# The low products of the next head's keys and values as 64-row tiles, with a chunk's halves in two PSUM banks

## What is computed

```
x = layernorm(x + self_attention(x))        # 16 heads of 16, 4 key/value groups, per sequence
x = layernorm(x + cross_attention(x, ctx))  # 8 heads of 128; all 1792 queries against all 6000 keys
x = layernorm(x + ffn(x))                   # 256 -> 1024 -> 256, ternary weights, exact gelu

# cross attention, for one head h
q = x @ Wq[:, h];  k = ctx @ Wk[:, h];  v = ctx @ Wv[:, h]      # 1792x128, 6000x128, 6000x128
sim = (q @ k.T) * 128 ** -0.5
sim = (sim - mean(sim)) * 1.5 + mean(sim)
out[:, h] = softmax(sim) @ v
```

## Time and profile before

| what | us |
|---|---|
| median of three executions | 2318.58 |
| profiled execution, its own time | 2320.05 |
| its span | 2318.2 |
| TensorE busy (28710 matmuls) | 2264.4 |
| VectorE busy | 2010.6 |
| GpSimd busy | 1893.1 |
| ScalarE busy | 1866.0 |

### The profile page before, as it was taken

How to read it: one execution, slowest core, us unless ns; L and a number is a source line. 1 busy time by engine, 2 the same in 40 slices (tenths; PEclk the granted TensorE clock), 3 DMA queues, 4 the chain that set the end, 5 groups by cost and what they waited for, 6 DMA issues and landing times.

```text
span 2318.2 us, 67173 instructions
## 1 busy us (share of the span) xinstructions
PE 2264.4 (98%) x28710; PEld 2025.3 (87%) x28710; DVE 2010.6 (87%) x2194; ACT 1866.0 (80%) x2220; POOL 1893.1 (82%) x1145
## 2 busy tenths in 40 slices
PE   7999999999999999999999999999999999999997
PEld 4568998899989998999889998999889998999885
DVE  7888888888889888888888888888898888988876
ACT  4357888888888888888888888888888888888854
POOL 8675888888878888888878897888878887899942
PEclk9999999999999999999999999999999999999999
DMA  6410000000000000000000000000000000010310
GB/s 201 155 38 15 7 4 13 4 7 6 11 6 5 7 13 4 6 4 7 13 4 7 4 13 4 6 7 4 13 4 6 7 4 7 4 47 7 110 59 33
DMA packets 34858, 50.79 MB, mean 22 GB/s; under 512 B 2304, under 2 KB 27392, under 8 KB 34560
## 3 DMA queue, kind: packets, MB, share of 16 engines
q1 hardware_dynamic: 34560, 46.46, 6.4%
HBM read 30.99 MB, written 15.47 MB: 20 GB/s over the span
## 4 chain that ended last, share of the span: by engine, by line
PE 70%; POOL 16%; DVE 5%; issue 4%; ACT 3%; POOLq 0%; ACTq 0%; DVEq 0%
PE psum L403 27%; POOL e_lo L1549 11%; PE psum L429 9%; PE psum L427 9%; PE psum L431 9%; PE psum L546 4%; PE psum L536 4%; POOL e_hi L1543 3%; DVE run_max L1045 3%; ACT ring L818 2%; PE psum L672 2%; PE psum L449 1%; PE psum L717 1%; PE psum L699 1%; PE psum L553 1%
## 5 line engine op out<-in xcount | busy, mean ns | idle before, releaser
L1549 POOL TENSOR_TENSOR e_lo<-ring,e_hi 128x1024 f16<-128x1024 f32 (+1 forms) x665 | 1389.5, 2105 | 197.0 <-ACT ring L833 168.4
L1045 DVE TENSOR_TENSOR run_max<-psum,run_max 128x1024 f16<-128x1024 f32 (+1 forms) x616 | 738.2, 1198 | 201.8 <-ACT ring L818 200.7
L818 ACT ACTIVATE ring<-psum 128x1024 f32<-128x1024 f32 (+1 forms) x672 | 674.4, 1004 | 181.5 <-PE psum L403 121.9
L1066 DVE SCALAR_TENSOR_TENSOR ring<-ring,psum 128x1024 f32<-128x1024 f32 (+1 forms) x672 | 792.6, 1186 | 0.7 <-PE psum L639 0.7
L403 PE MATMUL psum<-qx_hi,k_hi 128*128 128x256 f16 x2632 | 718.4, 273 | 13.9 <-DVE run_max L1045 7.7
L427 PE MATMUL psum<-v_main,e_hi 128*128 128x129 f16 x4032 | 717.7, 219 | 1.1 <-POOL e_lo L1549 1.1
L429 PE MATMUL psum<-v_main,e_hi 128*128 128x128 f16 x4032 | 718.3, 221 | 0.0
L403 PE MATMUL psum<-qx_hi,k_lo 128*128 128x256 f16 x2632 | 718.1, 273 | 0.0
L403 PE MATMUL psum<-qx_lo,k_hi 128*128 128x256 f16 x2632 | 718.0, 273 | 0.0
L431 PE MATMUL psum<-v_main,e_lo 128*128 128x129 f16 x4032 | 716.3, 218 | 0.0
L833 ACT ACTIVATE ring<-ring 128x1024 f32<-128x1024 f32 (+1 forms) x672 | 695.9, 1036 | 1.3 <-DVE ring L1066 0.8
(11 more groups left out here) (193 smaller groups left out, 2768.8 us busy)
## 6 DMA issues: line engine op xcount, KB each, us to landing
o_scratch<-o_buf SPq DMA_DIRECT2D x56, 128.0 KB, 1.9
raw<-o_scratch SPq DMA_DIRECT2D x14, 512.0 KB, 4.0
stage<-in_ctxT SPq DMA_DIRECT2D x6, 500.0 KB, 3.9
stage<-in_ctxT SPq DMA_DIRECT2D x12, 250.0 KB, 4.7
w_scratch<-wall SPq DMA_DIRECT2D x1, 2304.0 KB, 11.0
wall<-w_scratch SPq DMA_DIRECT2D x6, 384.0 KB, 3.2
x<-in_xT SPq DMA_DIRECT2D x4, 448.0 KB, 6.5
res<-in_x SPq DMA_DIRECT2D x1, 1792.0 KB, 15.8
```

Of the source, the lines that this page charges most:

```text
L818: a.activation(ring[:, f % SLOTS, 0:n], pair(f)[:, 0:n], ACT.Copy).then_inc(s_kept, 1)
L1045: ins = v.tensor_tensor(run_max[:, 0:n], pair(f)[:, 0:n], run_max[:, 0:n], ALU.max)
L1066: v.scalar_tensor_tensor(slot, slot, LIFT, psum[:, 6, 0:QB].unsqueeze(1).broadcast_to([P, t, QB]), ALU.add, ALU.subtract).then_inc(s_sub, 1)
L1549: g.tensor_tensor(e_lo[f % NEL][:, 0:n], slot, e_hi[f % NEH][:, 0:n], ALU.subtract).then_inc(s_lo, 1)
```

## The change

Keys: a chunk of 512 columns is made as two halves of 256 (`HC`). The products with `whi`, `wlo` and `wshi` are done once for each half. The product with `wslo` uses 64 rows of the array: rows 0 to 63 for the first half, rows 64 to 127 for the second. So that the high part of the context lies in the right rows, `ctx_s` is stacked the other way round in every second 256 keys (low parts in rows 0 to 63), and `wslo` holds the low weights in both halves of its rows, in place of the zeros. Values: of the four key tiles of a group, tiles 0 and 1 use rows 0 to 63, and tiles 2 and 3 use rows 64 to 127.

Where `two_banks(n, s)` holds (in the heads, at steps from 2 on, for full groups), the halves go to two banks: bank 7 and the output bank that the present block doesn't use. The two 64-row products stand next to each other. Elsewhere both halves are in bank 7, the two 64-row products are apart, and the second one waits for the end of the first (`s_rows`). ScalarE and VectorE read the two banks in two instructions each. TensorE waits for the output's store before it uses the borrowed bank (`s_oev`), and for the side tasks' end before a block's first `attend` (`s_free`); ScalarE stores the output earlier in its step, ahead of `keep_scores`. GpSimd works on context blocks of 1024 keys in place of 1000.

```diff
-CH = 1000
+CH = 1024
+HC = KC // 2
...
+        def two_banks(n, s):
+            what, index, h = side_of(n, s)
+            return what in ("k", "v") and n >= 0 and s >= 2 and tiles_of(index) == GT
+        def side_half(n, half):
+            return psum[:, (4 + (n + 1) % 2, 7)[half], 0:HC]
...
+                def key_product(banks, h, c, number=None):
                     whi, wlo, wshi, wslo = [wpack[h % 2][:, 4 + j, :] for j in range(4)]
-                    n = cols_of_keys(c)
-                    for x, (w, y) in enumerate(((whi, ctx_hi), (whi, ctx_lo), (wlo, ctx_hi),
-                                                (wshi, ctx_s), (wslo, ctx_s))):
-                        mm = pe.matmul(psum[:, bank, 0:n], lhsT=w, rhs=y[:, c * KC:c * KC + n],
-                                       start=(x == 0), stop=(x == 4))
+                    one = banks[0] == banks[1]
+                    def product(half, lhsT, y, start=False, stop=False, rows=None):
+                        k0, n = c * KC + half * HC, min(HC, cols_of_keys(c) - half * HC)
+                        of = slice(0, P) if rows is None else rows
+                        at_row = {} if rows is None else {"tile_position": (rows.start, 0)}
+                        return pe.matmul(psum[:, banks[half], one * half * HC:one * half * HC + n], lhsT=lhsT[of],
+                                         rhs=y[of, k0:k0 + n], start=start, stop=stop, **at_row)
+                    product(0, whi, ctx_hi, start=True)
+                    product(1, whi, ctx_hi, start=not one)
+                    if one:
+                        product(0, wslo, ctx_s, rows=rows_of(0)).then_inc(s_rows, 1)
+                    for half in range(2):
+                        product(half, whi, ctx_lo)
+                    for half in range(2):
+                        product(half, wlo, ctx_hi)
+                    if one:
+                        pe.wait_ge(s_rows, number)
+                        product(1, wslo, ctx_s, rows=rows_of(1))
+                    for half in range(2):
+                        mm = product(half, wshi, ctx_s, stop=one and half == 1)
+                    if not one:
+                        for half in range(2):
+                            mm = product(half, wslo, ctx_s, rows=rows_of(half), stop=True)
                     return mm
...
+                    def low(i):
+                        of = rows_of(i // 2)
+                        return pe.matmul(out_of(i), lhsT=ctx_s[of, keys_of(i)], rhs=wslo[of], start=False, stop=True,
+                                         tile_position=(of.start, 0))
+                    if one:
+                        for i in range(tiles_of(g)):
+                            whole(i)
+                            if i == 2:
+                                pe.wait_ge(s_rows, number)
+                            mm = low(i)
+                            if i == 1:
+                                mm.then_inc(s_rows, 1)
+                    else:
+                        for first in range(2):
+                            whole(first)
+                            whole(first + 2)
+                            low(first)
+                            mm = low(first + 2)
                     return mm
...
                     pe.wait_ge(s_free, number)
+                    if two_banks(n, s) and n > 0:
+                        pe.wait_ge(s_oev, n * QT + past * NQB * QT)
+                    banks = (4 + (n + 1) % 2, 7) if two_banks(n, s) else (7, 7)
...
                             pe.wait_ge(s_oev, n_at * QT - QT)
+                        if s == 0 and n >= 1:
+                            pe.wait_ge(s_free, number)
                         attend(n * NGRP + s, past * NQB * NGRP, past * HEAD_SIDES)
...
                         exp_half(weights)
+                    if s == 1 and n > 0:
+                        store_output(n - 1)
                     if f + LEAD < NF_ALL:
                         keep_scores(f + LEAD)
...
-                    if s == 1 and n > 0:
-                        store_output(n - 1)
...
-                for c in (7, 11):
-                    run(g.memset(wall[64:P, :, c, :], 0.0))
...
-                        run(g.tensor_tensor(wall[0:64, :, c + 3, :], rest[0:64], wall[0:64, :, c + 2, :],
-                                            ALU.subtract))
+                        run(g.tensor_tensor(wall[:, :, c + 3, :], rest, wall[:, :, c + 2, :], ALU.subtract))
...
-                        s_low = ctx_s[64:P, c0:c0 + CH]
-                        run(g.tensor_tensor(s_low, st[64:P, 1, 0:CH], s_low, ALU.subtract))
+                        for k0 in range(0, n, KC):
+                            for k, of in ((k0, slice(64, P)), (k0 + HC, slice(0, 64))):
+                                x = min(HC, n - k)
+                                s_low = ctx_s[of, c0 + k:c0 + k + x]
+                                run(g.tensor_tensor(s_low, st[of, 1, k:k + x], s_low, ALU.subtract))
```

More of the change, by code:

```diff
@@ L46 @@
 WA_N = WA_V + NG * DH_S
-CH = 1000
+CH = 1024
+NCH = -(-NKEY // CH)
 W12 = D * FF // P
@@ L224, in build @@
                  halves(INNER, Wk), halves(INNER, Wv)]
-        tasks += [halves(CH, ctxT[:, c * CH:(c + 1) * CH]) for c in range(NKEY // CH)]
+        tasks += [halves(min(CH, NKEY - c * CH), ctxT[:, c * CH:min((c + 1) * CH, NKEY)]) for c in range(NCH)]
         def maxima_bank(u):
@@ L265, in build @@
         s_side, s_half, s_free = sem("b_side"), sem("b_half"), sem("b_free")
+        s_rows = sem("b_rows")
         side16 = psum[:, 7, 0:QB // 2].bitcast(F16)
@@ L319, in build, with one_bank, rows_number @@
         HEAD_SIDES = side_number(NQB, 0) - side_number(0, 0)
+        def two_banks(n, s):
+            what, index, h = side_of(n, s)
+            return what in ("k", "v") and n >= 0 and s >= 2 and tiles_of(index) == GT
+        def one_bank(n, s, task):
+            return task[0] in ("k", "v") and not two_banks(n, s)
+        def rows_number(n, s):
+            return NGRP + sum((m, t) <= (n, s) and one_bank(m, t, task) for m, t, task in SIDES)
+        HEAD_ROWS = rows_number(NQB, -1) - rows_number(0, -1)
+        def side_half(n, half):
+            return psum[:, (4 + (n + 1) % 2, 7)[half], 0:HC]
         def v_of(h, g):
@@ L529, in norm_transposes, with rows_of @@
                     mm.then_inc(l_t, 1)
-                def key_product(bank, h, c):
+                def rows_of(half):
+                    return slice(64 * half, 64 * half + 64)
+                def key_product(banks, h, c, number=None):
                     whi, wlo, wshi, wslo = [wpack[h % 2][:, 4 + j, :] for j in range(4)]
-                    n = cols_of_keys(c)
-                    for x, (w, y) in enumerate(((whi, ctx_hi), (whi, ctx_lo), (wlo, ctx_hi),
-                                                (wshi, ctx_s), (wslo, ctx_s))):
-                        mm = pe.matmul(psum[:, bank, 0:n], lhsT=w, rhs=y[:, c * KC:c * KC + n],
-                                       start=(x == 0), stop=(x == 4))
+                    one = banks[0] == banks[1]
[21 more added lines that the diff above has]
+                            mm = product(half, wslo, ctx_s, rows=rows_of(half), stop=True)
@@ L538, in key_product, with value_product, out_of, keys_of @@
                     return mm
-                def value_product(bank, h, g):
+                def value_product(banks, h, g, number=None):
                     whi, wlo, wshi, wslo = [wpack[h % 2][:, 8 + j, :] for j in range(4)]
[L542 to L547, removed]
+                    one = banks[0] == banks[1]
+                    def out_of(i):
+                        return psum[:, banks[i // 2], (i if one else i % 2) * DH:(i if one else i % 2) * DH + DH]
+                    def keys_of(i):
+                        return slice((g * GT + i) * P, (g * GT + i + 1) * P)
+                    def whole(i):
+                        for x, (y, w) in enumerate(((ctx_hi, whi), (ctx_hi, wlo), (ctx_lo, whi), (ctx_s, wshi))):
+                            pe.matmul(out_of(i), lhsT=y[:, keys_of(i)], rhs=w, start=(x == 0), stop=False)
+                    def low(i):
[16 more added lines that the diff above has]
+                            mm = low(first + 2)
@@ L565, in start_task @@
                     if what == "k":
-                        pe.wait_ge(s_staged, 3 + min(-(-(index + 1) * KC // CH), NKEY // CH))
-                        key_product(7, 0, index).then_inc(st_full, 1)
+                        pe.wait_ge(s_staged, 3 + -(-(index + 1) * KC // CH))
+                        key_product((7, 7), 0, index, index + 1).then_inc(st_full, 1)
                     else:
@@ L614, in side @@
                     pe.wait_ge(s_free, number)
+                    if two_banks(n, s) and n > 0:
+                        pe.wait_ge(s_oev, n * QT + past * NQB * QT)
+                    banks = (4 + (n + 1) % 2, 7) if two_banks(n, s) else (7, 7)
+                    order = rows_number(n, s) + past * HEAD_ROWS
```

(30 more changed lines are left out.)

11 lines of the change are left out of this document (6 added, 5 removed).

## The result

The changed kernel takes 2384.01 us (median of four executions, 2383.74 to 2385.48) against 2319.36 for the kernel before. The ratio is 1.0277 (95% interval 1.0264 to 1.0289): slower by 64.7 us. The forecast was 2373.0, +54.4 us, and 2384 lies inside its range of 2346 to 2388. The direction and the mechanism held; the sum was 10 us short. A head that holds no loop jump grew by 6.96 to 7.06 us (from its first `attend` to the next head's); the forecast was 6.5.

A forecast was written before the change was run, and what follows sets the result against it. The prediction took TensorE to bound the kernel, with each round trip into row tiles costing 0.19 us; its terms summed to 54.4 us, giving 2373.0 us from a median of 2318.58, range 2346 to 2388.

The forecast's parts named there:

- products in the heads: Key chunks and value groups in the heads: 4.6 + 13.7 + 21.6 + 4.6 us slower, from round trips into row tiles.
- self attention and values before the first head: Products standing alone before the heads: 3.5 us more for 12 key chunks, 4.2 us for 9 value groups.
- evacuations: Split ScalarE and VectorE copies out of two banks: 0.31 us once per head where line 536 waits, 2.2 us in all.
- store, s_oev, s_free, s_rows: The output's store moved earlier and TensorE's new waits before borrowed banks, blocks and rows: cost 0.
- rival C: Pairs of 64-row products run in turn, not side by side: 13.6 us on top of the forecast, 2386.6; chance 0.05.
- The bound: Time added on TensorE inside a head lands on the span one for one; ScalarE or VectorE time is free without deadlines.
- The price of a trip: Leaving the plain array for row tiles and returning costs TensorE 0.18 to 0.19 us; 0.19 taken.
- Rival B: No charge for 64-row tiles, so pairs win: 10.5 us faster, 2308.1; chance 0.08.
- Before the first head: Nine value groups alone, partly filling TensorE's gap of about 0.7 us: some 0.85 per two steps, 4.2 us in all.

The follow-up runs named there:

- e1_full_rows: The changed kernel with each 64-row product done on all 128 rows, everything else kept: 2327.18 us, ratio to before 1.0036.
- e2_one_trip: The changed kernel, but a two-bank value group does all 128-row products first, then its four 64-row ones, entering the tiles once: 2368.74 us, ratio 1.0209.
- e6_before_key64: The kernel before, with only the last product of each key chunk on rows 0 to 63; no halves, pairs or second bank: 2338.31 us, ratio 1.0075.
- e3_same_rows: The changed kernel with both products of a pair on the same rows, leaving out the second half's low-weight term: 2394.77 us, ratio 1.0331.
- e5_alone_full: The changed kernel with the 64-row products that stand alone done on all 128 rows, pairs kept on row tiles: 2355.65 us, ratio 1.0152.
- e7_store_late: The changed kernel with the output's store back at its old place, after the exponentials of step 1: 2406.04 us, ratio 1.037.
- e4_unrolled: The changed kernel with TensorE's hardware loop over heads 2 to 5 written out: 2375.2 us, ratio 1.0242.
- e9_before_unrolled: The kernel before with only TensorE's loop over heads 2 to 5 written out: 2315.83 us, ratio 0.9984.

## Why the prediction was right, and where it was short

The sum of the prediction and what the traces show, in us:

| term | forecast | measured | from |
|---|---|---|---|
| products in the heads | 44.5 | 50.7 | lengths of the groups, 49.2, and 0.011 for the product after each of 136 |
| self attention and values before the first head | 7.7 | 8.1 | first `attend` of head 0, 211.46 - 203.37 |
| evacuations | 2.2 | -0.4 | what is left; the wait for the keys' low part got 0.4 shorter |
| store, s_oev, s_free, s_rows | 0 | 0 | no such wait in the view of waits |
| jump of TensorE's loop | 0 | 5.3 | last block of head 3 and first of head 4, against those of other heads |
| clock at the end | 0 | 1.7 | half clock for 3.4 us from 2364.1, in this profiled execution, not in that of the kernel before |
| sum | 54.4 | 65.4 | spans, 2383.6 - 2318.2 |

The forecast's range reached 2388 for rival C's sake, not for the loop's. That 2384 still lies in it, with 7.0 us for which the sum had no term, is in part luck.

**The bound.** It held, nearly one for one, that time added on TensorE lands on the span. From e1_full_rows to the changed kernel the product groups in the heads cost 49.1 us more and the heads grew by 47.8; most of the rest came out of old waits for low parts. Before the heads it was 9.1. The two give 56.9, the medians 56.8.

**The price of a trip: right mechanism, size a little low.** I took 0.19 us from 32-row tiles. The changed kernel shows, from the start of one product to the next (the trace has them to the ns), 0.152 into the tile where 0.056 is due (entry 0.096), 0.159 out of it (exit 0.103), and 0.067 for the next product (0.011): 0.21, and e2_one_trip 0.213. I had seen the 0.01 and named it, and left it out of the sum. The heads have 301 trips; 0.023 more for each is 6.9 us, about the missing 6.2.

Since the price of 0.213 doesn't depend on what is done in the tiles, the best unit of this change, a key chunk as a pair, can save 0.107 and still loses 0.104. The value group needs two trips to save twice 0.053. The products that stand alone save nothing, and cost half of the whole.

**Rival B.** The switch has a price, 0.21 us a trip (e2_one_trip, e6_before_key64), so rival B falls. The Trainium skill, TensorEngine Tiling (Array Packing), Key Properties, says that changing the tiling mode drains the engine. The traces agree in that each change costs time, 0.096 us in and 0.103 out. The 2x of that page's section Theoretical Speedup, in the Trainium skill, is seen for the product itself (two in the time of one, against e3_same_rows), not for the kernel.

**Evacuations.** The term of 2.2 us was wrong. Its price was too high to begin with, since I added full row lengths. A row of ScalarE or VectorE runs on while the next one has begun; what it takes of the engine is the distance to the next start. One copy of 512 columns before, then two of 256 after, each with the row that follows:

```profile
883.54 0.59 ACT L850 ACTIVATE k_hi<-psum 128x512 f16<-128x512 f32 x1
884.01 1.06 ACT L833 ACTIVATE ring<-ring 128x1024 f32<-128x1024 f32 x1
```

```profile
255.33 0.66 ACT L932 ACTIVATE v_main<-psum 128x256 f16<-128x256 f32 x2
255.85 1.07 ACT L916 ACTIVATE ring<-ring 128x1024 f32<-128x1024 f32 x1
```

That is 0.52 against 0.47, 0.05 more and not 0.17. VectorE's low parts take 0.66 against 0.60, 0.06 more and not 0.14. And the wait of line 568 went from 3.5 to 3.1 us: TensorE itself arrived later by the price of its tiles (with the tiles taken out, in e1_full_rows, it is 3.9), so the old stall took it up.

**The loop.** Nothing in the prediction spoke of it. The row was in the trace of before (the 2.8 us, the longest of 11 waits on `run_max` in the earlier trace rows), and I took it for a wait on VectorE. It is the jump of the hardware loop. It is 2.85 us from product to product before, 3.08 in e6_before_key64, which has exactly as many products as before, and 5.4 to 5.9 in the changed kernel and in all its versions that keep the loop. The view of DMA queues shows what the doubled gap holds. The kernel before, 1221.5 to 1224.4 us, then the changed kernel, 1257.5 to 1263.2 (queue, kind: packets, MB, share):

```profile
q8 instruction: 1, 0.02, 2.2%
```

```profile
q8 instruction: 2, 0.03, 2.1%
```

Each is a transfer of 16 KB of instructions. The first starts 0.1 us after the last product of the body, and where there is a second, it starts 3.1 to 3.4 us later. The gap of the kernel before and that of e6_before_key64 hold one, those of the changed kernel, e1, e2, e3, e5 and e7 two. In e4_unrolled and e9_before_unrolled no two of them start within 7 us of each other (300 to 2100 us), and no gap appears. The short gap goes with one transfer and the long one with two in a row, in all eight traces that have the jump; that TensorE waits for them is likely by this, not shown. Why the changed body needs the second is open; it is longer and has more waits, and no run separates the two. What follows a gap is shown: half clock in all of these but the kernel before, for 3.4 us in e7_store_late and for 6.8 in the others.

**Before the first head.** The forecast let the alternate groups fill a gap of 0.7 in a cycle of two steps and took 0.85 for the two. The cycle went from 5.6 to 5.8 us (5.78 in the earlier trace rows, 172.87 - 167.09) to 7.0. Here is the start of one product run in each of two cycles of the changed kernel, from its chain:

```profile
171.72 0.33 PE psum L603 x4
...
178.73 0.33 PE psum L603 x4
```

TensorE became the bound there altogether. It's 1.2 to 1.4 per cycle, not 0.85. The table's 8.1 flatters the term: in the kernel before, this stretch held 3.4 us of half clock (from 199.1 us) that the changed kernel did not have. Against e1_full_rows, with the same half clock there as the changed kernel, it is 9.1.

## What to carry to other kernels

Row tiles pay only where a stay in them saves more than a round trip costs, 0.21 us here: about 500 columns' worth of TensorE's time at full clock. Count the trips, not the tiles, and put all tile products of a stage together. An estimate from these numbers: a pair of 128 columns saves 0.053, so a stay breaks even at four such pairs. No version here reached that; the two of e2_one_trip still lose. A 64-row product alone between full ones saved nothing here and cost a whole trip (e5_alone_full, e6_before_key64). When a TensorE-bound kernel with a hardware loop shows one odd long wait, look where in the program it stands, and at the instruction queue in the DMA view, before believing the engine that is named.

## What the runs showed that I had not expected

- The jump of TensorE's loop: 2.85 us from product to product in the kernel before with one transfer of instructions in it, 5.7 in the changed one with two, and there 6.8 us at 1.2 GHz. Written out, the loop gives back 8.8 us in the changed kernel and 3.7 in the one before.
- The entry and exit of 64-row tiles cost the same as those of 32-row tiles and 32-column tiles: 0.096 and 0.103 us, against 0.09 and 0.09 in the earlier trace rows.
- Inside the mode, pairs follow each other without any charge: four 64-row products of 128 columns in 0.29 us, tails included.
